# Reset quarter in front of the second half state, and ten groups of input products moved, in a GRU chain on one core

## The reference

```python
z = sigmoid(x_t @ W_z + h @ U_z + v_z)
r = sigmoid(x_t @ W_r + h @ U_r + v_r)
hh = tanh(x_t @ W + (r * h) @ U + v)
h = (1 - z) * h + z * hh          # output of step t; x = x + h
```

## Time and profile before

| | us |
|---|---|
| timed runs | 952.94, 953.34, 956.28 (median 953.34) |
| profiled execution, its own time | 952.06 |
| its span, first to last instruction | 950.3 |
| stretch of the two recurrences | about 18 to 575 |
| PE busy | 902.5 (95%) |
| DVE busy | 842.4 (89%) |
| ACT busy | 595.2 (63%) |
| POOL busy | 217.3 (23%) |

### The profile page before, as it was taken

One profiled execution on the slowest core, in us unless ns is written; L12 is line 12 of the kernel. 1 busy time (PEld: TensorE's weight loads), 2 busy tenths in 40 slices (PEclk: granted clock), 3 DMA queues, 4 the chain that ended last, 5 costly groups with the idle time before them and its releaser, 6 DMA issues.

```text
span 950.3 us, 96702 instructions
## 1 busy us (share of the span) xinstructions
PE 902.5 (95%) x42718; PEld 717.9 (76%) x42718; DVE 842.4 (89%) x3139; ACT 595.2 (63%) x2606; POOL 217.3 (23%) x430
## 2 busy tenths in 40 slices
PE   5899999999999999999999998699999999999997
PEld 5799999999999999999999994255555555555555
DVE  3799999989999998998999994999999999999993
ACT  3577777777777777777777773345555555455552
POOL 0011111111111111111111112333433344434340
PEclk9999999999999999999999999889999999999999
DMA  5031331331001010010010100001100000001001
GB/s 183 27 103 47 127 116 41 110 113 39 25 28 36 28 36 28 25 39 25 25 39 28 36 17 22 10 1 40 35 25 25 25 25 25 25 25 49 26 26 44
DMA packets 38005, 41.46 MB, mean 44 GB/s; under 512 B 5088, under 2 KB 31200, under 8 KB 36832
## 3 DMA queue, kind: packets, MB, share of 16 engines
q1 hardware_dynamic: 36832, 40.55, 13.2%
q10 hardware_dynamic: 1152, 0.66, 0.2%
HBM read 32.28 MB, written 8.91 MB: 43 GB/s over the span
## 4 chain that ended last, share of the span: by engine, by line
PE 52%; DVE 34%; issue 9%; ACT 3%; DMA 2%; DVEq 0%; ACTq 0%; SPq 0%
PE bank L784 19%; PE bank L837 18%; PE bank L769 12%; DVE arena L698 11%; DVE early L717 4%; DVE early L708 4%; DVE none_h L629 4%; ACT cand_kept L405 3%; DVE early L721 2%; DVE early L715 2%; DVE early L696 2%; DVE early L702 2%; PE bank L945 1%; PE bank L916 1%; DMA beta<-in_beta 1%
## 5 line engine op out<-in xcount | busy, mean ns | idle before, releaser
L290 POOL TENSOR_TENSOR x<-x_f,h_f 128x64 f32 x256 | 84.8, 331 | 499.4 <-PE bank L784 498.2
L945 PE MATMUL bank<-x,wl 128*128 (+1 forms) x384 | 181.0, 610 | 0.9 <-DVE rank_rows L675 0.9
L769 PE MATMUL bank<-x_ahead,early 128*32 128x64 f32 x8256 | 171.6, 220 | 3.7 <-ACT bank L363 2.0
L837 PE MATMUL bank<-none_h,early 128*32 128x32 f32 x8192 | 154.2, 199 | 14.9 <-DVE none_h L629 3.0
L784 PE MATMUL bank<-early,none_h 128*32 128x64 f32 x4096 | 165.4, 223 | 0.8 <-issue 0.8
L405 ACT ACTIVATE cand_kept<-bank 128x32 f32<-128x32 f32 x512 | 99.1, 201 | 99.0 <-PE bank L837 99.0
L629 DVE TENSOR_TENSOR_SCAN none_h<-zero_z,cand_kept 128x64 f32<-128x64 f32 x512 | 123.6, 283 | 35.7 <-ACT cand_kept L405 6.9
L837 PEld LDWEIGHTS bank<-none_h,early 128*32 128x32 f32 x8192 | 116.9, 110 | 38.4 <-DVE none_h L629 32.7
L769 PEld LDWEIGHTS bank<-x_ahead,early 128*32 128x32 f32 x8256 | 140.1, 110 | 5.1 <-DMA x_ahead<-in_x 3.0
L945 PEld LDWEIGHTS bank<-x,wl 128*128 128x128 f32 x384 | 68.6, 190 | 88.1 <-issue 88.1
L837 PE MATMUL bank<-rh_f,early 128*32 128x32 f32 x8192 | 130.2, 199 | 2.1 <-issue 1.9
(11 more groups left out here) (107 smaller groups left out, 1607.9 us busy)
## 6 DMA issues: line engine op xcount, KB each, us to landing
x_ahead<-in_x SPq DMA_DIRECT2D x130, 64.0 KB, 1.8
x_in<-in_x SPq DMA_DIRECT2D x32, 256.0 KB, 2.7
arena<-in_w SPq DMA_DIRECT2D x8, 1024.0 KB, 6.4
out<-y SPq DMA_DIRECT2D x32, 256.0 KB, 2.4
rank_rows<-in_bias_rows SPq DMA_DIRECT2D x1, 1024.0 KB, 6.2
arena<-scratch SPq DMA_DIRECT2D x64, 16.0 KB
early<-in_cx SPq DMA_DIRECT2D x1, 768.0 KB, 4.5
early<-in_wx SPq DMA_DIRECT2D x1, 768.0 KB, 6.3
```

What stands on the lines that cost most here:

```text
L290: pool.tensor_tensor(x2[:, :, :, s], x1_f[:, u % LOOP], h1_f[:, u % 2], ALU.add).then_inc(x2_done, 1)
L769: mm = pe.matmul(out[32 * j:32 * j + 32], weights(k, j, m), moving(k), start=False, stop=False, tile_position=(0, 32 * j), skip_group_chec ...
L837: mm = pe.matmul(out[32 * j:32 * j + 32], weights(k, j, m), moving(k), start=False, stop=k == 1, tile_position=(0, 32 * j), skip_group_che ...
L945: mm = pe.matmul(banks[(at + 2 * par) % 4][:], wl2[:, k, mat, unit], x2[:, k, bass.ds(p * GB, GB), :].rearrange("p q t -> p (q t)"), start ...
```

## The change

It touches the PE's program alone. Within a step the reset quarter k0 to m1 goes directly behind k0 to m0, in front of the wait for the second half of the state, and behind a new wait for the second candidate tanh of the step before (`cand_done`, against a value worked out from the loop's counter n). The update gate's half k0 goes behind all reset quarters. The input products in front of U go from 40 to 32: in an even step eight of them go behind `second_inputs` (32 become 40 behind the second gate), in an odd step eight go behind the second gate (16 become 24). No product is added or taken away.

```diff
-            def ahead_update(par, v):
-
-                return by_rows(pre_z[par][:, v, :], lambda k: x_ahead[:, par, v, k, :], lambda k, j: wx[:, k, j, 1, :])
+            def ahead_update(par, v, parts=range(HALVES)):
+
+                return by_rows(pre_z[par][:, v, :], lambda k: x_ahead[:, par, v, k, :], lambda k, j: wx[:, k, j, 1, :],
+                               parts)
...
-            def first_gates(u):
+            def first_gates(n, u):
...
                 pe.wait_ge(h_done, 1)
                 reset(0, 0)
-                update(0)
+                pe.wait_ge(cand_done, n * 2 * LOOP + 2 * u + 1)
+                reset(0, 1)
                 pe.wait_ge(h_done, 2)
                 reset(1, 0, taken=h_done).then_inc(r_pre, 1)
-                reset(0, 1)
                 reset(1, 1).then_inc(r_pre, 1)
+                update(0)
                 update(1).then_inc(z_pre, 1)
...
-            def even(u):
+            def even(n, u):
...
                 ahead_first(nxt, 0, 1)
-                ahead_first(nxt, 2, 0, (0,))
                 first_cand(u)
                 second_gate(u)
                 second_inputs((LOOP - STEPS, 0)[par], nxt)
-
-            def odd(u):
+                ahead_first(nxt, 2, 0, (0,))
+
+            def odd(n, u):
...
-                ahead_update(nxt, 0).then_inc(update_seeded, -1)
+                ahead_update(nxt, 0, (0,)).then_inc(update_seeded, -1)
                 first_cand(u)
                 second_gate(u)
+                ahead_update(nxt, 0, (1,))
                 ahead_update(nxt, 1).then_inc(ahead_loaded[nxt], -16)
...
-            with nc.Fori(0, T // LOOP, engines=bass.OrderedEngineSet([pe.engine]), hint_back_edge=True):
-                turn()
+            with nc.Fori(0, T // LOOP, engines=bass.OrderedEngineSet([pe.engine]), hint_back_edge=True) as n:
+                turn(n)
```

More of the change, by code:

```diff
@@ L879, in second_inputs @@
                 ahead_second(at, par).then_inc(x1_ready, -STEPS)
-            def even(u):
+            def even(n, u):
                 par, nxt = u // STEPS, 1 - u // STEPS
-                first_gates(u)
+                first_gates(n, u)
                 pe.wait_ge(ahead_loaded[nxt], 16)
@@ L898, in odd, with turn @@
                 pe.wait_ge(update_seeded, 1)
-                ahead_update(nxt, 0).then_inc(update_seeded, -1)
+                ahead_update(nxt, 0, (0,)).then_inc(update_seeded, -1)
                 first_cand(u)
                 second_gate(u)
+                ahead_update(nxt, 0, (1,))
                 ahead_update(nxt, 1).then_inc(ahead_loaded[nxt], -16)
[L904 to L908, removed]
+            def turn(n):
+                even(n, 0)
+                odd(n, 1)
+                even(n, 2)
+                odd(n, 3)
             def adapter_rows(w):
```

## The result

| | before | after |
|---|---|---|
| timed runs, median (us) | 954.81 (4 runs) | 964.10 (962.71 to 965.60, 4 runs) |
| ratio of after to before | | 1.0097, 95% interval 1.0072 to 1.0122 |
| profiled execution: its own time, its span | 952.06, 950.3 | 962.71, 960.9 |

The change makes the kernel 9.3 us slower, about 1.0%. The forecast was 962. Its total was right and its place was wrong: it put the loss into the steps in the middle of a turn, and these did not get slower. That the totals agree is luck.

What follows compares the result with a forecast made beforehand. Latency inside a step bounds the kernel, the update path 0.02 us behind the candidate path. Normal steps + 7.7 us, back edge 1 and 0.6, make + 9: 961.1 profiled, 962 as median; range 950 to 975.

Steps and rivals of the forecast that it cites:

- back edge: Step behind the loop's branch, one in four: 1 us from its own delays plus 0.6 us from the later branch.
- update path: From the last z products through z sigmoid, transpose, L639 and L619 to the scan; + 0.04 us per step, 7.7 in 192.
- Order, + 0.050: z's first half moved behind the reset quarters: 0.113 more less 0.063 makes z_pre and the scan 0.050 us later.
- Wait, + 0.01: The new wait's register instruction among the gates, taken at 0.01 us per step on the update path.
- The upper and the lower bound: Start of the reset quarters behind the new wait: 0.02 to 0.05 us later at most, 0.01 earlier at least.
- the prediction's sign: Place of the 16 reset products behind the first eight: under 0.20 covered, 0.21 to 0.25 as bounded, more is dear.
- The price that the prediction took from rows of two waits at one product (304.40): On PE, a separate 51 ns wait between the last z product (304.40) and the inputs (304.52): 0.12 us.
- Room, 0.02: The update path stands only 0.02 us behind the candidate path; this distance is subtracted from the step's loss.
- candidate path's 0.06: Reset gate through r * h, U and tanh to the scan comes 0.06 us earlier, gaining nothing beyond 0.02 unless z does.
- faster rival: The candidate path decides alone if the update path has more room: 0.06 in 256 steps, 15 us, 938; chance 0.12.
- dear rival: Two register instructions or one at the loop's head: + 18 to + 22 us, 973; chance 0.15.
- Inputs behind the second gate: Eight more products before the next gates in even steps, covered by 0.02 us; uncovered, up to 0.05 in 128 steps, 6 us.

Runs made afterwards that it cites:

- kernel 1: Changed kernel with the new wait against a constant, on a semaphore of its own that PE takes back (DVE and ACT wait for it too): ratio 0.9991 to before.
- kernel 6: Changed kernel with the register wait moved ahead of the wait for the state, in front of the gates: ratio 1.0210 to before.
- kernel 7: kernel 1 with a second, long fulfilled register wait in front of U's own wait: ratio 1.0129 to before.
- kernel 8: Changed gates with constant wait and old inputs, z's first half back in front of the wait for the second half of the state: ratio 1.0025 to before.
- Kernel 5: kernel 1 plus a long fulfilled register wait between the input products, so the loop reads its counter: ratio 1.0016 to before.
- Kernel 3: Kernel before with only the inputs regrouped: 32 in front of U, 40 and 24 behind the second gate: ratio 1.0081 to before.
- kernel 2: Kernel before with only the register wait added, in front of the reset quarter k0 to m1 where it stood: ratio 1.0050 to before.
- kernel 11: Changed kernel with the PE's turn made of eight steps instead of four: 1742.69 us, ratio 1.8245 to before.
- 4: kernel 1 with 40 inputs in front of U again, the input products as before: ratio 1.0047 to before.
- 9: As kernel 8, but only two of the four column blocks of z's first half in the wait: ratio 1.0083 to before.
- 10: kernel 1 with 40 and 16 inputs in the last step of a turn: ratio 0.9990 to before.

## Why the prediction was right and wrong

**The total and the sign** were right: 962 forecast, 964.1 measured, slower by over 0.5%. The total is right by luck: 7.7 us too much in the normal steps and 7.8 too little at the back edge cancelled.

**The place was wrong.** The forecast laid 7.7 of its 9 us on the 192 normal steps. These stayed at 2.10. The step that failed is the sum on the update path, "+ 0.050 (order) + 0.01 (wait) - 0.02 (its distance now)":

- *Order, + 0.050: mis-sized.* The last z product moved from 0.859 to 0.872 behind the scan (medians), by 0.013. From the last reset product to the last z product it was 0.123 before and is 0.203 after: eight more z products in a row cost 0.080, not the 0.113 of eight input products. The last reset product came 0.067 earlier, against 0.063 in the sum.
- *Wait, + 0.01: nothing.* No run shows this 0.01; the runs showed 0.01 the other way. The upper and the lower bound were 0.02 to 0.05 later and 0.01 earlier; it is the lower. The 16 reset products behind the state's second half start 0.537 behind the scan, 0.547 before; that is 0.19 or 0.16 behind the first eight, under the 0.20 of the prediction's sign. Kernels 1 and after have their last reset products at 0.668 and 0.670 in normal steps. The register instruction was not over before the state arrived: the trace shows it 0.362 to 0.367 behind the scan in all 168 normal steps, beside the gates' first product (0.347 or 0.373), where the first scan ends at 0.29. It makes the early quarter later, 0.457 against 0.431 to 0.443 in kernel 1, but the quarter behind that one waits for the second half of the state anyway and swallows it. The price that the prediction took from rows of two waits at one product (304.40) belongs to another case: there, as in kernels 6 and 7, the second wait is an instruction of its own, 51 ns long. The 0.09 on ACT is the pitch of short activations (kernel 8: 0.953, 1.047, 1.139).
- *Room, 0.02: right, and enough.* Of the 0.013 the z sigmoid passed on 0.008: before, it started 0.094 behind the second r sigmoid (1.053 and 1.147), at ACT's own pitch, so z's products had some ns of room. L619 to the scan went from 0.345 to 0.330 in the median. + 0.012 - 0.015 is nothing. Of the signs that were named for being right, the step of 2.13 to 2.15 and the z sigmoid 0.05 later did not come (2.10, and 0.01 later).

**The candidate path's 0.06** arrived and was wasted, as forecast: U 0.05, the tanh 0.06 earlier, the second r sigmoid 0.09 behind the first, L619 to the scan 0.33. The faster rival fell for the reason given.

**The back edge** was taken at 1.6 us and cost 9.4. The prediction did see it, "if a register instruction is put at the loop's head too, it is up to 0.12 in 64 steps, 7.7 us", and left it in the dear rival. Kernel 5, which reads the counter and has the copy at the loop's head, lies 3.1 us over kernel 1, and the register instruction in the middle of the gates costs the rest (6.0 us). In a normal step the products behind the wait for the second half of the state start at 0.537 after and at 0.53 in kernel 1, so that wait hides it. Behind the branch and the copy the first product starts at 0.51, the register instruction at 0.54 (medians), the ninth product at 0.64: the second scan ended at 0.48, and no wait is left to hide it. The diff said that the counter is read, and the rows showed that the gates behind the branch start late (0.39 against 0.35); these together should have put the term into the sum. The dear rival's 18 to 22 us do not come out of its terms either: 9, 0.03 to 0.05 in 192 steps, and 7.7 are 22 to 26.

**Inputs behind the second gate**: they cost nothing, but they were not covered as forecast. In the steps behind an even one the gates start 0.373 behind the scan, in the others 0.347, so the eight products do reach into the gates by 0.026. The early quarter stands in the wait for the second half of the state and takes it up, and the last reset product is at 0.67 in both. Kernel 3 shows what the cover is worth when it is gone: (0.032 + 0.049) x 64 = 5.2 us in its steps 1 and 3, where 6 was forecast.

**A term that nobody had**: step 1 is 0.012 longer after than before and 0.025 longer than in kernel 1. Its cause is shown in the last section, a scan that meets POOL's addition; 12 times 0.14 is 1.7 us. What brings the two together is open.

## What to carry to other kernels

In a loop bound by latency, price the step behind the loop's branch by itself: what the sequencer does there was not hidden here (that step went from 2.286 to 2.433 us), though the same wait cost nothing in the other steps (2.10 in both), where a later wait swallowed it. A wait against a constant, with a semaphore that the consumer takes back, was worth 1% here against one on the loop's counter, and brought no more than the kernel before had. And when two paths of a step end together, a shift that shortens one is worth nothing until the other is shortened too: look first at which of the two is ahead, and by how much.

## What the runs showed of the hardware

- A register instruction behind an open wait did not start before the wait had ended: in the kernel after it starts 0.362 to 0.367 behind the scan (the first scan ends at 0.29), in kernel 2 0.55 behind (the second ends at 0.48). Among products with no open wait in front, 0.86 or 0.95 behind the scan, it left the normal step at 2.10 (kernel 5).
- With four steps of 320 instructions on PE in the loop's body, the whole run moved 10 packets on the queue for instructions; with eight steps it moved 357, 10 to 12 in every turn, and a turn was 24.6 us longer than two turns of four; the branch in it was 2.2 us long instead of 0.22 (kernel 11).
- Where two waits stood in front of one PE instruction, an EVENT_SEMAPHORE of 51 ns stood at the second, and the product came 0.07 to 0.09 later in kernel 6 (0.44 behind the scan against 0.35 to 0.37) and 0.11 later in kernel 7, where the first wait was long fulfilled (1.48 against 1.37).
- The two r sigmoids and the z sigmoid followed each other by 0.093 in the median in kernel 8, although each is 0.20 to 0.22 long.
- DVE's second scan and POOL's addition were longer, 0.41 for 0.27 and 0.38 for 0.33, where they overlapped. The step behind a back edge after, and a normal one, DVE and POOL:

```profile
366.99 0.62 DVE L629 TENSOR_TENSOR_SCAN none_h<-zero_z,cand_kept 128x64 f32<-128x64 f32 x2
...
367.15 0.33 POOL L290 TENSOR_TENSOR x<-x_f,h_f 128x64 f32 x1 [2.06 <-PE bank L784]
...
310.25 0.38 POOL L290 TENSOR_TENSOR x<-x_f,h_f 128x64 f32 x1 [1.72 <-PE bank L784]
```

The second scan starts 0.21 behind the first. Where POOL starts 0.16 behind the first, ahead of the second, that scan takes 0.41 instead of 0.27; where POOL starts 0.23 behind, the addition takes 0.38 instead of 0.33. Whichever starts second is longer, by 0.14 or 0.05; it does not wait until the first is done. The first case happens in one step of sixteen at most: 12 times between steps 40 and 250 after, 7 times before, 13, 5 and 2 times in kernels 6, 3 and 2, and never in the seven kernels whose DVE waits against the constant (1, 4, 5, 7, 8, 9, 10). That POOL's early start follows from a late back edge is not borne out: kernel 7 has a late one (2.405) and no such scan, the kernel before an early one and seven. DVE's own wait on the counter goes with it, and was not tried by itself.
